# Second cross attention of a six-stage decoder: softmax division moved ahead of the transposes

## What is computed

```python
q = split_heads(Q @ W_Q + b_Q)          # 16 heads of 8, from x
k = split_heads(K @ W_K + b_K)          # from the context, 77 rows
v = split_heads(V @ W_V + b_V)
scores = einsum('bhqd,bhkd->bhqk', q, k) / sqrt(8)
weights = softmax(scores, axis=-1)
out = einsum('bhqk,bhkd->bhqd', weights, v)
return out (heads joined) @ W_O + b_O
```

## Time and profile before

| | |
|---|---|
| Median of 3 runs | 2057.4 us (2054.84 to 2058.22) |
| Profiled execution, its time | 2057.52 us |
| Profiled execution, its span | 2055.5 us |
| TensorE matmul busy | 1695.4 us (82% of the span) |
| VectorE busy | 1273.8 us (62%) |
| ScalarE busy | 1203.0 us (59%) |
| GpSimd busy | 399.5 us (19%) |

### The profile page before, as it was taken

How to read it: one execution, slowest core, us unless ns; L and a number is a source line. 1 busy time by engine, 2 the same in 40 slices (tenths; PEclk the granted TensorE clock), 3 DMA queues, 4 the chain that set the end, 5 groups by cost and what they waited for, 6 DMA issues and landing times. The chain is left out here.

```text
span 2055.5 us, 31160 instructions
## 1 busy us (share of the span) xinstructions
PE 1695.4 (82%) x11522; PEld 986.2 (48%) x11522; DVE 1273.8 (62%) x1804; ACT 1203.0 (59%) x2497; POOL 399.5 (19%) x369
## 2 busy tenths in 40 slices
PE   3999999999999446888875748999999995888861
PEld 1444444444434125666653324666666664666651
DVE  0777777777777368777345424666666664566627
ACT  2777877777777326777821525555555553466533
POOL 0111111011011036666400001222222221110000
PEclk9999999999999656888965869999999997899985
DMA  4000000000000000000000010000000000000001
GB/s 118 1 11 1 0 11 0 0 0 0 0 1 0 8 16 4 8 2 1 2 3 0 0 42 1 1 1 1 1 1 1 1 2 13 11 8 5 2 3 41
DMA packets 36377, 16.66 MB, mean 8 GB/s; under 512 B 15286, under 2 KB 35088, under 8 KB 36240
## 3 DMA queue, kind: packets, MB, share of 16 engines
q1 hardware_dynamic: 32080, 8.91, 2.0%
q10 hardware_dynamic: 4160, 5.90, 0.8%
HBM read 12.71 MB, written 2.10 MB: 7 GB/s over the span
## 5 line engine op out<-in xcount | busy, mean ns | idle before, releaser
L1985 POOL TENSOR_TENSOR self_probs<-self_probs,self_rz 128x1024 f32<-128x1024 f32 x64 | 121.3, 1895 | 548.6 <-DVE self_rz L2013 548.6
L1960 ACT ACTIVATE self_probs<-self_scores,self_neg 128x128 f32<-128x128 f32 x512 | 181.4, 384 | 16.7 <-DVE self_neg L2008 16.7
L525 POOL TENSOR_SCALAR gru_decay<-gru_zgate 128x512 f32<-128x512 f32 x96 | 75.5, 787 | 591.7 <-ACT gru_zgate L478 566.4
L389 PE MATMUL gru_gate<-gru_xn,gru_whg 128*128 128x512 f32 x384 | 182.6, 598 | 3.5 <-DVE gru_xn L568 3.5
L393 PE MATMUL gru_hid<-gru_xn,gru_whg 128*128 128x512 f32 x384 | 181.4, 595 | 0.0
L401 PE MATMUL gru_out<-gru_y,gru_wo 128*128 128x512 f32 x384 | 178.1, 599 | 0.7 <-DVE gru_y L596 0.7
L1016 PE MATMUL x_turned<-const_ident,x_probs 128*77 128x128 f32 x1024 | 156.8, 302 | 11.5 <-ACT x_pt L1118 9.4
L1118 ACT ACTIVATE x_pt<-x_turned 77x512 f32<-77x512 f32 x224 | 122.3, 583 | 64.7 <-PE x_turned L1016 64.4
L1016 PEld LDWEIGHTS x_turned<-const_ident,x_probs 128*77 128x77 f32 x1024 | 128.3, 163 | 61.7 <-issue 28.5
L1210 DVE TENSOR_REDUCE x_m<-x_scores 128x16 f32<-128x1232 f32 x64 | 92.0, 1437 | 94.3 <-PE x_scores L1005 94.1
L591 DVE SCALAR_TENSOR_TENSOR gru_ghid<-gru_hid,gru_half_c,gru_sighid 128x512 f32<-128x512 f32 x96 | 71.8, 747 | 114.6 <-ACT gru_sighid L479 114.5
(11 more groups left out here) (347 smaller groups left out, 3550.3 us busy)
## 6 DMA issues: line engine op xcount, KB each, us to landing
gru_whg<-in_L_attn_Whg ACTq DMA_DIRECT2D x4, 768.0 KB, 10.1
x_ctx_in<-in_ctx SPq DMA_DIRECT2D x16, 154.0 KB
gru_xin<-in_x SPq DMA_DIRECT2D x8, 256.0 KB, 2.9
out<-moe_res SPq DMA_DIRECT2D x8, 256.0 KB, 2.3
gru_wo<-in_L_attn_Wo ACTq DMA_DIRECT2D x4, 384.0 KB, 11.0
self_w_raw<-in_L_attn_Wq SPq DMA_DIRECT2D x1, 512.0 KB, 6.0
self_w_raw<-in_L_attn_Wk ACTq DMA_DIRECT2D x1, 512.0 KB, 6.7
self_w_raw<-in_L_attn_Wv SPq DMA_DIRECT2D x1, 512.0 KB, 9.1
```

The lines of the kernel that those rows point to most:

```text
L389: mm(ps_gate[n % 2][:, :], whg[:, l, k, DI + c * P:DI + (c + 1) * P], xn[u][:, k, :], start=(k == 0), stop=(k == KH - 1))
L1960: last = f(probs[n % 2][:, a, jj, :], ps_s[n % 2][:, a, jj * T:(jj + 1) * T], ACT.Exp, bias=neg[n % 2][:, a, jj:jj + 1], accum_out=z[n % 2 ...
L1985: pool.tensor_tensor(probs[n % 2][:, :, :, :], probs[n % 2][:, :, :, :], whole, ALU.mult).then_inc(pn_ready.sem, 1)
```

## The change

Only stage `x1` changes; wherever `temper` is set, all stays. Four things:

1. The second half of `attend`, the multiplications with `x_zpad`, is left out, and with it `logs`. `zpad`, `logz` and `rz` are no longer made.
2. A new step `weigh`, in slot n for sequence n-1: VectorE sums each head's exponentials (`x_zsum`, 128x16 from 128x1232) and takes the reciprocal (`x_zinv`), and GpSimd multiplies `x_probs` in place by it. `turn` step 0 waits for that product (`weighed`) in place of `p_ready`. `scale` becomes a copy by ScalarE.
3. `turn` is spread over two slots: steps 0 and 1 run two slots after the scores, steps 2 and 3 and `attend` three slots after. `x_probs` gets a third buffer. ScalarE empties all four steps.
4. The places in the shared bank are moved, and `square` and `divide` with them.

```diff
-        TURNED_BY_DVE = () if temper else (3,)
-        LE, LT, LA = (7, 8, 9) if temper else (0, 1, 2)
+        LE, LT, LA = (7, 8, 9) if temper else (0, 2, 3)
+        PRING = 2 if temper else 3
...
-            PLACES = [(("context", 1), ("keys", 1)), (("queries", 1), ("values", 1)), (None, None), (("mix", -1), ("var", -1))]
+            PLACES = [(("var", -2), ("context", 1)), (("keys", 1), ("queries", 1)), (("values", 1), None), (("mix", -1), None)]
...
+            if not temper:
+
+                ORDER += [("scores", n, 0), ("kbd", n + 1, 0), ("weigh", n - 1, 0)]
+                ORDER += [("square", g - 2, 0)] * (r == 0)
+                ORDER += [("turn", n - LA, 2), ("turn", n - LA, 3)] + place(n, 0, False) + place(n, 0, True)
+                ORDER += [("divide", g - 2, 0)] * (r == 0)
+                ORDER += [("turn", n - LT, 0), ("turn", n - LT, 1), ("attend", n - LA, 0), ("exp", n - LE, 0)]
+                ORDER += [("scale", n - LA, 0)] + place(n, 1, False) + place(n, 1, True)
+                continue
...
                     elif kind == "turn":
                         if c == 0:
-                            pe.wait_ge(p_ready.sem, n + 1)
+                            pe.wait_ge((p_ready if temper else weighed).sem, n + 1)
...
-                        for part in range(2):
+                        for part in range(2 if temper else 1):
...
+                    elif kind == "scale" and n % 2 and not temper:
+                        act.wait_ge(a_mm.sem, n + 1)
+                        if n >= 2 * GB:
+                            act.wait_ge(misc_mm.sem, MISC["mix", n // GB - 2] + 1)
+                        at = n // 2 % 2 * 2 * T
+                        f(oT[n // GB % 2][:, at:at + 2 * T], ps_a[:, 0:2 * T], ACT.Copy).then_inc(o_ready.sem, 1)
...
+                    elif kind == "weigh":
+                        pool.wait_ge(zinv_ready.sem, n + 1)
+                        r = zinv[n % 2][:, :].unsqueeze(2).broadcast_to([P, H, S])
+                        pool.tensor_tensor(probs[n % PRING][:, :, :], probs[n % PRING][:, :, :], r, ALU.mult).then_inc(weighed.sem, 1)
...
-                    elif kind == "turn" and c in TURNED_BY_DVE:
+                    elif kind == "weigh":
+                        dve.wait_ge(p_ready.sem, n + 1)
+                        v.tensor_reduce(zsum[:, :], probs[n % PRING][:, :, :], AX.X, ALU.add).then_inc(zsum_ready.sem, 1)
                         if n >= 2:
-                            dve.wait_ge(a_mm.sem, n - 1)
-                        dve.wait_ge(t_mm[c].sem, n + 1)
-                        v.tensor_copy(pt[n % 2][:, c, :, :].rearrange("p j t -> p (j t)"), ps_t[c % 2][0:S, :]).then_inc(pt_ready[c].sem, 1)
+                            dve.wait_ge(weighed.sem, n - 1)
+                        dve.wait_ge(zsum_ready.sem, n + 1)
+                        v.reciprocal(zinv[n % 2][:, :], zsum[:, :]).then_inc(zinv_ready.sem, 1)
```

More of the change, by code:

```diff
@@ L774, in cross_attention @@
         vpad = t.sb("vpad", [S, VRING, GB, H, ROWS])
-        zpad = t.sb("zpad", [S, TILE4, ROWS])
         kbd = [t.sb(f"kbd{r}", [P, TILE4, S]) for r in range(2)]
@@ L778, in cross_attention @@
         dist = t.sb("dist", [P, RING, H, S])
-        probs = [t.sb(f"probs{r}", [P, H, S]) for r in range(2)]
+        probs = [t.sb(f"probs{r}", [P, H, S]) for r in range(PRING)]
         pt = [t.sb(f"pt{r}", [S, TILE4, TILE4, T]) for r in range(2)]
-        logz = t.sb("logz", [P, 2 * T])
-        rz = t.sb("rz", [P, 2 * T])
         oT = [t.sb(f"oT{r}", [P, GROUP]) for r in range(2)]
@@ L800, in cross_attention @@
             half = t.sb("half", [P, 1])
+            zpad = t.sb("zpad", [S, TILE4, ROWS])
+            logz = t.sb("logz", [P, 2 * T])
+            rz = t.sb("rz", [P, 2 * T])
             e1 = [t.sb(f"e1_{r}", [P, H, S]) for r in range(2)]
@@ L805, in cross_attention @@
             g1, g2, lt, rt = (t.sb(n, [P, GB * H]) for n in ("g1", "g2", "lt", "rt"))
+        else:
+            zsum = t.sb("zsum", [P, H])
+            zinv = [t.sb(f"zinv{r}", [P, H]) for r in range(2)]
         loaded = t.count("loaded", weight=DMA)
@@ L821, in cross_attention @@
         a_mm = t.count("a_mm")
-        logz_ready = t.count("logz_ready")
-        rz_ready = t.count("rz_ready")
         o_ready = t.count("o_ready")
@@ L843, in cross_attention @@
             pre_ready = t.count("pre_ready")
+            logz_ready = t.count("logz_ready")
+            rz_ready = t.count("rz_ready")
+        else:
+            zsum_ready = t.count("zsum_ready")
+            zinv_ready = t.count("zinv_ready")
+            weighed = t.count("weighed")
         if temper:
@@ L864, in cross_attention @@
             g, r = n // GB, n % GB
-            ORDER += [("scores", n, 0), ("kbd", n + 1, 0)] + [("pre", n - LE, 0)] * bool(temper)
+            if not temper:
[6 more added lines that the diff above has]
+                continue
+            ORDER += [("scores", n, 0), ("kbd", n + 1, 0), ("pre", n - LE, 0)]
             ORDER += [("turn", n - LT, 0), ("turn", n - LT, 1), ("logs", n - LA - 1, 0), ("scale", n - LA - 1, 0)]
-            ORDER += [("divide", g - (4 if temper else 2), 0)] * (r == 0)
+            ORDER += [("divide", g - 4, 0)] * (r == 0)
             ORDER += place(n, 0, False) + place(n, 0, True)
-            ORDER += [("soft", n, 0), ("sums", n - 1, 0)] * bool(temper) + [("exp", n - LE, 0)] * (not temper)
+            ORDER += [("soft", n, 0), ("sums", n - 1, 0)]
             ORDER += [("turn", n - LT, 2), ("turn", n - LT, 3)]
-            ORDER += [("square", g - (3 if temper else 1), 0)] * (r == 3)
-            ORDER += [("exp", n - LE, 0)] * bool(temper) + [("attend", n - LA, 0)]
+            ORDER += [("square", g - 3, 0)] * (r == 3)
+            ORDER += [("exp", n - LE, 0), ("attend", n - LA, 0)]
             ORDER += place(n, 1, False) + place(n, 1, True)
-            if temper:
-                ORDER += [("feat", g - 1, 0)] * (r == 0) + [("mean", g, 0), ("rate", g - 1, 0)] * (r == 2)
-        PER_SEQ = ("scores", "pre", "turn", "sums", "attend", "logs", "scale", "soft", "exp", "kbd")
+            ORDER += [("feat", g - 1, 0)] * (r == 0) + [("mean", g, 0), ("rate", g - 1, 0)] * (r == 2)
+        PER_SEQ = ("scores", "pre", "turn", "sums", "attend", "logs", "scale", "soft", "exp", "kbd", "weigh")
         ORDER = [s for s in ORDER if 0 <= s[1] < (B if s[0] in PER_SEQ else NG)]
@@ L923, in _ @@
                                    pattern=[[DK, H]], channel_multiplier=-1).then_inc(padded.sem, 1)
[L924 to L928, removed]
+                if temper:
+                    pool.wait_ge(padded.sem, 2)
+                    pool.memset(zpad[:, :, :], 0.0).then_inc(padded.sem, 1)
+                    pool.wait_ge(padded.sem, 3)
+                    for i in range(TILE4):
+                        pool.memset(zpad[:, i, i * DK:(i + 1) * DK], 1.0)
             @block.vector
@@ L1015, in _ @@
                         for j in range(TILE4):
-                            last = turn_(ps_t[c % 2][0:S, j * T:(j + 1) * T], probs[n % 2][:, TILE4 * j + c, :], ident[:, :])
+                            last = turn_(ps_t[c % 2][0:S, j * T:(j + 1) * T], probs[n % PRING][:, TILE4 * j + c, :], ident[:, :])
                         last.then_inc(t_mm[c].sem, 1)
@@ L1109, in _ @@
                         else:
-                            if n >= 2:
-                                act.wait_ge(t_mm[TILE4 - 1].sem, n - 1)
+                            if n >= PRING:
+                                act.wait_ge(t_mm[TILE4 - 1].sem, n - PRING + 1)
                             act.wait_ge(d_ready.sem, n + 1)
-                            f(probs[n % 2][:, :, :], dist[:, n % RING, :, :], ACT.Exp, scale=DK ** -0.5).then_inc(p_ready.sem, 1)
-                    elif kind == "turn" and c not in TURNED_BY_DVE:
+                            f(probs[n % PRING][:, :, :], dist[:, n % RING, :, :], ACT.Exp, scale=DK ** -0.5).then_inc(p_ready.sem, 1)
+                    elif kind == "turn":
                         if c == 0 and n >= 2:
@@ L1242, in _ @@
                         v.tensor_scalar(lt[:, :], lt[:, :], LOG_T_MAX, None, ALU.min).then_inc(lt_ready.sem, 1)
-                    elif kind == "scale" and n % 2:
+                    elif kind == "scale" and n % 2 and temper:
                         dve.wait_ge(rz_ready.sem, n // 2 + 1)
```

## The result

The changed kernel takes 2038.4 us (median of 4 runs, 2036.88 to 2042.25), the kernel before 2057.4 (4 runs, 2054.84 to 2058.22): ratio 0.991, 95% interval 0.9895 to 0.993, 19 us less. The forecast was 2028, 29.5 less. Faster, as forecast, but the gain was put half as large again as it came out.

The account below looks back on a forecast made before the run. TensorE's queue, by work and holes, was taken to bound the kernel at 26.76 us a group. With groups at 21.7, 31.2 us saved less 1.4 at the ends gave 29.8 off 2057.5, about 2028 us, range 2017 to 2039.

Parts of the forecast that it names:

- its first: Whole kernel: stages run one after another, so the changed stage's saving, 29.8 us, comes off the total in full.
- TensorE, 29 us of sums off it: TensorE in the changed stage: sums go, 3.6 us a group, 29 over 32 sequences, leaving 19.4 a group.
- VectorE's slot: VectorE in the changed stage: 4.48 us a slot plus 2.17 once a group, 20.1 a group by itself.
- The chain: Slots 0 and 1: turning waits for GpSimd's product, with queries and scores queued behind; 10.67 us, 11.19 with contention.
- the lock: `divide` beside GpSimd's product in slot 0: the two exclude each other, costing 0.52 us once a group.
- Sum of the period: `x_m` of sequence 4 to that of 31: 146.8 us against 178.0 before, 31.2 saved.
- The two ends: Changed stage up to sequence 4: nothing taken; after `x_m` of 31: 1.4 us lost, between 0 and 4.
- VectorE alone: Rival, changed stage: chain and lock cost nothing, VectorE sets a group of 20.1 us; total 2016 us, chance 0.12.
- holes that stay: Rival, TensorE's queue: each of 27 slots has half a us more than counted; total 2041 us, chance 0.20.
- exclusion of the two engines: Rival: no VectorE work runs during GpSimd's, a slot 8.0 us against 6.69; total 2094 us, chance 0.04.
- The signs of being right: Changed stage: slots of about 21.7 us a group, first pair longest, VectorE's scores wait some 15 us, TensorE waiting for GpSimd's product.

Follow-up runs that it names:

- Experiments 5 and 6: One idle TensorE product ending each turn of the last stage's first loop: 5 in the changed kernel, 2025.8 us; 6 in the kernel before, 2055.4 us.
- experiment 9: Changed kernel's order, but sums of exponentials left on TensorE with Ln, Exp and VectorE's product, no `weigh`: 2040.5 us in one run.
- 11 and 12: Changed kernel with queries early in slot 2, `divide` ahead of the sum in slot 1, idle product in the last stage's loop: 2021.7, then 2021.3 us.
- experiment 7: Changed kernel with `divide` moved from slot 0 to slot 1, ahead of the sum: 2026.9 us in one run.
- experiment 3: Kernel before with five idle TensorE products while the last stage's weights load, ahead of its loop: 2066.1 us, ratio 1.0047.

## Why the prediction was wrong

- **The step that failed is its first**: "The six stages run one after another, so what this stage saves the kernel saves." The unchanged last stage took 12.7 us more, at a lower TensorE clock. Its first loop has two courses, 32 to 35 us and 44 to 47 for the same instructions. In the fourteen profiles here the last stage takes 77.6 to 80.8 us nine times and 90.0 to 92.4 five times; the kernel before was on the fast course and the changed one on the slow. Experiments 5 and 6 show the 12.7 us to be that: with the pause filled the last stage is 79.5, and the two kernels lie 29.6 us apart (good to about 4) against 29.8 forecast. I had asked only whether the clock would fall within the changed stage. There it stayed at 1.00 over the periods, and was lower only in the first and last groups (0.95 over the whole stage, 0.98 before). Why the changed kernel enters the last stage so that it takes the slow course stays open.
- **TensorE, 29 us of sums off it**: right as work, but most of the gain comes without it. With the sums kept in the new order, a group is 22.8 (experiment 9). The forecast named the holes of the old order (3.8 a group) only in a rival; closing them, taken first, is five sixths of the gain.
- **VectorE's slot**, 4.48 and 2.17 a group: slots 2 and 3 forecast at 5.31 and 5.22, measured 5.26 and 5.41. The 0.2 in slot 3 is the wait of `x_m` behind `x_y`'s own signal (0.21 in each group), which I left out. The reciprocal took 0.25, as taken.
- **The chain**: slots 0 and 1 forecast 11.19, measured 11.34. Two terms were off and cancel, which is luck: the queries cost 1.06 from start to start where I had 0.86, and the lock 0.31 and not 0.52. In the kernel before, the weight loads of the queries start 0.10 ahead of their matmuls, and those of the turning behind them start ahead too. Here the loads of the queries and of the scores start together with their matmuls. The 0.15 left is turning at 1.03 (0.95 taken), `attend` at 1.01 (0.98) and the product starting 0.04 later.
- **Sum of the period**: six groups and three slots 146.8, measured 147.8. **The two ends**: up to sequence 4, nothing taken, 2.4 lost (22.7 against 20.3); after the last maximum 1.4 loss taken, 1.1 gained. The two errors cancel, so that 28.8 came so near to 29.8 by luck in part. The second profile of this kernel shares it out otherwise: 20.3, then 149.1, then 22.4 (0.1 gained), and a stage of 191.7 all the same.
- **Rivals**: VectorE alone and holes that stay did not come; exclusion of the two engines came as one product in four, 0.31 us, and as one `divide` of 1.40. The signs of being right came in the stage: the first pair of slots the longest, `x_m` waiting 17.3 us for scores, the turnings waiting for the product.
- **Range and signs**: the median lay within 2017 to 2039, at its edge, but for a reason that the range did not contain.

## What to carry to other kernels

A changed stage can alter the course of an unchanged one behind it, so compare the granted clock of every later stage before adding up. Here a loop that pauses 1.31 us in each turn of 10.21 stayed at 1.2 GHz for its whole length. One idle product in that pause kept 22 of the 23 runs with it (experiments 5, 6, 11 and 12; the other is the one of 2871 us) clear of the slow totals, where idle products ahead of the loop made one kernel slower. And before moving work off the busiest engine, count its holes: here reordering the queue brought 3.97 us a group, and moving the sums after that 0.77.

## What the runs showed of the hardware beyond that

By the totals, the same kernel ran on either course from run to run: with the queries moved, 2014.8 and 2038.0; with the loop entered later, three fast and six slow. At the low clock the loop repeated its 10.21 us turn unchanged to its end (46.8 us), with TensorE busy 35.6 of them. With one idle product a turn (1.06 us at the low clock) the clock was up at the start of the second turn (the same eight instructions 1.87 us in the first, 1.06 in the second), but it was so in experiment 7 as well, without any. Entering at the high clock did not keep it: in experiment 3 the clock fell within the first turn, and the three turns after it ran at the low one.

`divide` on VectorE and the product on GpSimd held each other up, whichever came second: by 0.31 us for the product, by 0.77 for the `divide` that started 1.40 us into a product of 2.25.
